# Self attention values with high and low probabilities in one matmul of 512 columns, bank halves added on VectorE, and both queries ahead of the projections

## The reference

```python
q = (x @ wq.T).reshape(b, l, NH, HD)
k = (x @ wk.T).reshape(b, l, NKV, HD)
v = (x @ wv.T).reshape(b, l, NKV, HD)
q = apply_rope(q, freqs_cos, freqs_sin)
k = apply_rope(k, freqs_cos, freqs_sin)
k_full = jnp.concatenate([k_sel, k[0]], axis=0)     # 16 * 32 cached rows and 64 new ones: 576 keys
v_full = jnp.concatenate([v_sel, v[0]], axis=0)
scores = jnp.einsum('bhld,bhtd->bhlt', qh, k_full) / math.sqrt(HD)
attn = jax.nn.softmax(scores, axis=-1)
out = jnp.einsum('bhlt,bhtd->bhld', attn, v_full)
return out.transpose(0, 2, 1, 3).reshape(b, l, NH * HD) @ wo.T
```

## Time and profile before

| | |
|---|---|
| median of 3 runs | 2754.13 us |
| lowest, highest | 2749.89, 2757.01 us |
| the profiled execution | 2757.09 us |
| its span on the core | 2755.3 us |
| mean granted TensorE clock | 0.992 of full speed |
| instructions in the trace | 64145 |
| matmuls, weight loads | 26496, 26496 |
| of them in the self attention's values (L1954) | 13824 each |
| VectorE, ScalarE, GpSimd busy | 1998.2 us (73%), 1538.0 us (56%), 1621.8 us (59%) |

### The profile page before, as it was taken

How to read it: one execution, slowest core, us unless ns; L and a number is a source line. 1 busy time by engine, 2 the same in 40 slices (tenths; PEclk the granted TensorE clock), 3 DMA queues, 4 the chain that set the end, 5 groups by cost and what they waited for, 6 DMA issues and landing times.

```text
span 2755.3 us, 64145 instructions
## 1 busy us (share of the span) xinstructions
PE 2695.3 (98%) x26496; PEld 2374.7 (86%) x26496; DVE 1998.2 (73%) x4005; ACT 1538.0 (56%) x3207; POOL 1621.8 (59%) x1379
## 2 busy tenths in 40 slices
PE   6999999999999999999999999999999999999997
PEld 6888988998888888888888888888888888888876
DVE  5666666666666676666666678887778878777887
ACT  5566666666666566655656655554445455444445
POOL 6887887888777667666667763233334433333235
PEclk8999999999999999999999999999999999999998
DMA  5233233323325312322231331111112111111111
GB/s 172 80 81 106 85 86 100 96 71 104 108 61 166 91 48 80 87 70 77 80 91 44 86 101 43 35 54 35 47 38 64 50 43 39 50 35 43 31 31 62
DMA packets 91484, 197.71 MB, mean 72 GB/s; under 512 B 20664, under 2 KB 21304, under 8 KB 89144
## 3 DMA queue, kind: packets, MB, share of 16 engines
q1 hardware_dynamic: 71480, 154.80, 20.3%
q10 hardware_dynamic: 17664, 34.61, 3.9%
q0 software_dynamic: 2048, 4.20, 0.5%
HBM read 176.78 MB, written 16.78 MB: 70 GB/s over the span
## 4 chain that ended last, share of the span: by engine, by line
PE 89%; DVE 6%; POOL 2%; ACT 2%; issue 1%; DMA 0%; ACTq 0%; DVEq 0%
PE big L1862 30%; PE bank L1862 30%; PE big L1934 14%; PE bank L1954 12%; PE big L1954 3%; DVE nmx L1417 1%; DVE P L1423 1%; PE big L1855 0%; POOL ptl L799 0%; DVE xol L1514 0%; POOL oTl L804 0%; DVE P L1687 0%; DVE rall L1439 0%; DVE qTl L1412 0%; ACT P L972 0%
## 5 line engine op out<-in xcount | busy, mean ns | idle before, releaser
L799 POOL TENSOR_TENSOR ptl<-P,pth 128x576 fp32r<-128x576 f32 x512 | 724.8, 1434 | 240.2 <-ACT pth L981 239.4
L972 ACT ACTIVATE P<-big,nmx 128x576 f32<-128x576 f32 x512 | 378.5, 739 | 406.2 <-DVE nmx L1417 406.0
L1423 DVE STREAM_TRANSPOSE P<-P 128x576 f32<-128x576 f32 x512 | 387.8, 767 | 150.2 <-ACT P L972 148.0
L1954 PE MATMUL bank<-pth,v 32*128 32x256 f32 x4608 | 424.5, 281 | 4.6 <-DVE xacc L1445 1.7
L1954 PE MATMUL big<-pth,v 32*128 32x256 f32 x4608 | 424.6, 281 | 0.0
L1954 PEld LDWEIGHTS bank<-pth,v 32*128 32x128 f32 x4608 | 384.2, 187 | 17.0 <-issue 14.2
L1417 DVE TENSOR_REDUCE nmx<-big 128x1 f32<-128x576 f32 x512 | 373.3, 747 | 6.6 <-PE big L1934 4.8
L981 ACT ACTIVATE pth<-P 128x576 fp32r<-128x576 f32 x512 | 347.7, 682 | 51.0 <-DVE P L1423 50.7
L1954 PEld LDWEIGHTS big<-pth,v 32*128 32x128 f32 x4608 | 363.2, 187 | 0.0
L880 POOL TENSOR_TENSOR P<-P,sm 128x512 f32<-128x512 f32 x64 | 67.3, 1051 | 486.9 <-DVE sm L1716 486.9
L1954 PE MATMUL bank<-ptl,v 32*128 32x256 f32 x2304 | 351.5, 278 | 0.0
(11 more groups left out here) (283 smaller groups left out, 8014.6 us busy)
## 6 DMA issues: line engine op xcount, KB each, us to landing
rall<-kept_r ACTq DMA_DIRECT2D x64, 512.0 KB, 3.7
raw<-in_wo SPq DMA_DIRECT2D x64, 256.0 KB, 3.4
raw<-in_xWq SPq DMA_DIRECT2D x64, 256.0 KB, 2.8
raw<-in_xWo SPq DMA_DIRECT2D x64, 256.0 KB, 2.8
raw<-in_wq SPq DMA_DIRECT2D x62, 256.0 KB, 3.0
v<-kept_v SPq DMA_DIRECT2D x24, 448.0 KB, 7.3
v<-kept_v SPq DMA_DIRECT2D x68, 128.0 KB, 3.4
raw<-in_xWkv SPq DMA_DIRECT2D x32, 256.0 KB, 2.9
```

Of the source, the lines that this page charges most:

```text
L799: pool.tensor_tensor(third_columns(ptl, i), blocks_of(i), f(third_columns(pth, i)), ALU.subtract).then_inc(p_low(i), 1)
L972: act.activation(P[:, i % PSLOTS, :].rearrange("p (k n) -> p k n", k=2), ps_s[i % 2][:, :, 0:HALF], ACT.Exp, bias=nmx[:, i % 8:i % 8 + 1], ...
L1423: dve.transpose(P[:, i % PSLOTS, :], P[:, i % PSLOTS, :]).then_inc(p_turned(i), 1)
L1954: m = pe.matmul(ps_o[a][:, 0:256], v[r, s, l, :], p[r, lo:hi + 1:hi - lo, block_of(b), :, :], start=first, stop=final)
```

## The change

It has four parts.

1. **Probabilities.** `pth` and `ptl` become halves of one tile `pt` [128, 2, 3, KB, 4, 32]. A block now takes two rounds: the high values times high and low probabilities at once, 512 columns, a whole bank; and the low values times the high probabilities, 256 columns, into the bank's first half. 144 matmuls and weight loads a group instead of 216, with the same number of columns.
2. **Adding the halves.** A new step `sum_out(k, a)` on VectorE reduces the two halves of bank a to 256 columns in a new tile `osum` (two slots), and frees the bank (signal `o_sum`). `normalise_out` then reads `osum` and `rall`, both in SBUF.
3. **Room.** `VSLOTS` goes from 22 to 20, so `VEARLY` from 4 to 2: 16 blocks are late instead of 14.
4. **Order.** PE does query 1 and score 7 ahead of projection 0, scores 8' and 9' around projection 1, and the small task between projections 2 and 3. ScalarE does exponential 5 ahead of the high parts of outputs 2 and 3, the query's high parts earlier, exponential 7 after high part 6 and query high 1. VectorE does maxima 4 and 5 between the sums and normalisations, query low 1 before add 0. GpSimd's order and SP's are as they were.

```diff
 GROUPS = 64
-VSLOTS = 22
+VSLOTS = 20
 VEARLY = VSLOTS - KB
...
-            pth, ptl = pair("pt", [128, 3, KB, 4, 32], one)
+            pt = sb("pt", [128, 2, 3, KB, 4, 32], F32R, one)
+            pth, ptl = pt[:, 0], pt[:, 1]
             qTh, qTl = pair("qT", [128, 2, 512], one)
             oh, ol = pair("oT", [128, 2, 512], one)
             rall = sb("rall", [128, 8, 128], F32, one)
+            osum = sb("osum", [128, 2, 2, 4, 32], F32, one)
...
                     out_hi(k, 1)
                 if after:
                     exponent(8 * (k + 1) + 4)
+                if after:
+                    exponent(8 * (k + 1) + 5)
                 if now:
                     out_hi(k, 2)
                     out_hi(k, 3)
+                if later:
+                    query_hi(k + 2, 0)
                 if after:
-                    exponent(8 * (k + 1) + 5)
                     turned_hi(8 * (k + 1) + 4)
                     turned_hi(8 * (k + 1) + 5)
-                if later:
-                    query_hi(k + 2, 0)
                 if 0 <= g < G - 1 and c == 2:
                     values_hi(g + 1)
                 if after:
...
-            def normalise_out(k, a):
+            def sum_out(k, a):
+
                 gate.wait_ge(pv_done, k)
                 gate.wait_ge(in_r, k)
-                dve.tensor_tensor(rall_quarter(a), ps_o[a][:, 0:256].rearrange("p (u t j) -> p u t j", u=2, t=4),
-                                  rall_quarter(a), ALU.mult).then_inc(o_norm((k, a)), 1)
+                both = ps_o[a].rearrange("p (l u t j) -> p u t j l", l=2, u=2, t=4)
+                if k >= 1 or a >= 2:
+                    gate.wait_ge(o_norm, (k, a - 2) if a >= 2 else (k - 1, a + 2))
+                dve.tensor_reduce(osum[:, a % 2], both, AX.X, ALU.add).then_inc(o_sum((k, a)), 1)
+
+            def normalise_out(k, a):
+                gate.wait_ge(o_sum, (k, a))
+                dve.tensor_tensor(rall_quarter(a), osum[:, a % 2], rall_quarter(a), ALU.mult).then_inc(
+                    o_norm((k, a)), 1)
...
-                        normalise_out(k, a)
+                    sum_out(k, 0)
+                    sum_out(k, 1)
+                    normalise_out(k, 0)
+                    normalise_out(k, 1)
+                if after:
+                    maximum(8 * (k + 1) + 4)
+                if now:
+                    sum_out(k, 2)
+                    sum_out(k, 3)
+                if after:
+                    maximum(8 * (k + 1) + 5)
+                if now:
+                    normalise_out(k, 2)
+                    normalise_out(k, 3)
                 if k == GROUPS - 1:
...
 
+            p_rows = pt.rearrange("p h s b t j -> p h s (b t j)")
...
-                    out_place(a, (o_norm, (k, a)))
+                    out_place(a, (o_sum, (k, a)))
                 lo, hi = sorted((slot(k, 0), slot(k, 1)))
                 for b in range(KB):
                     s = (KB * n + b) % VSLOTS
-                    for j, (l, p) in enumerate(((0, pth), (1, pth), (0, ptl))):
+                    o = 128 * block_of(b)
+                    for l in range(2):
                         for a in range(4):
                             r = slice(32 * a, 32 * a + 32)
-                            first, final = b == 0 and j == 0, b == KB - 1 and j == 2
-                            m = pe.matmul(ps_o[a][:, 0:256], v[r, s, l, :], p[r, lo:hi + 1:hi - lo, block_of(b), :, :], start=first,
-                                          stop=final)
+                            first, final = b == 0 and l == 0, b == KB - 1 and l == 1
+                            p = p_rows[r, 0:2 - l, lo:hi + 1:hi - lo, o:o + 128]
+                            m = pe.matmul(ps_o[a][:, 0:512 - 256 * l], v[r, s, l, :], p, start=first, stop=final)
                             if final and a == 3:
                                 m.then_inc(pv_done(k), 1)
...
                     query(k + 2, 0)
                 if after:
                     score(8 * (k + 1) + 6)
+                if later:
+                    query(k + 2, 1)
+                    score(8 * (k + 1) + 7)
                 if now:
                     project(k, 0)
-                if after:
+                if after and not later:
                     score(8 * (k + 1) + 7)
+                if later:
+                    score(8 * (k + 2))
                 if now:
                     project(k, 1)
-                if later:
-                    score(8 * (k + 2))
-                if later:
-                    query(k + 2, 1)
-                for a in task(k):
-                    small_task(*a)
```

52 lines of the change are left out of this document (25 added, 27 removed).

## The result

The changed kernel takes 2781.08 us (median of 4 runs, 2775.78 to 2782.99) against 2754.54 us for the kernel before: a ratio of 1.0099, 95% interval 1.0084 to 1.0113, so 26.5 us slower. The prediction was 2770 us, slower.

A forecast was written before the change was run, and what follows sets the result against it. PE, busy 98% of the span, was taken to bound the kernel. Terms -12.5 + 19.3 + 5.4 + 4.8 + 1.3 - 2.4 = +15.9 us gave 2770 us against the median of 2754.1; range 2746 to 2788.

The forecast's parts named there:

- forecast A: The prediction itself: slower, with GpSimd late in the gathering groups as main loss; 2770 us, own range 2763 to 2778, chance 0.47.
- Rival B: GpSimd is late in the gathering groups, but the shared port is harmless: 2760 us, chance 0.19.
- rival C: In the values, weight loads rather than columns pace PE, and a third are gone: faster, 2739 us, chance 0.16.
- Rival E: In the values, long rounds save only by the gap of 2.5 ns, the rest as forecast A: 2780 us, chance 0.05.
- term 1: Values on PE: merged rounds save 0.24 us a group, in 52 of 64 groups, -12.5 us.
- Term 3: GpSimd's low parts start 1.95 us later behind ScalarE's exponential 5; PE waits in twelve gathering groups, +19.3 us.
- Term 2: VectorE's four new adds take a step of 0.60 us and cost PE nothing, with 0.5 us to spare.
- rival D: VectorE's adds are slow, at a step of 1.13 us, and PE waits: some +90 us, 2840 us, chance 0.13.
- Term 4: VectorE's normalisations of two SBUF tensors wait for GpSimd: +5.4 us in value gatherers, +4.8 in groups 29, 30, 31, 61.
- term 5: Ends: +1.3 us after the last values, -2.4 us in group 1, nothing for the smaller value ring.

The follow-up runs named there:

- Experiment 5: The changed kernel with two of the four gathers moved on GpSimd between output low 1 and output low 2: 2753.88 us, ratio 1.0010.
- Experiment 2: The changed kernel with normalisations 2 and 3 again ahead of maximum 5, and high parts of outputs 2 and 3 ahead of exponential 5: 2786.7 us.
- experiment 3: The changed kernel's new order with the values and normalisation of the kernel before, without adds, ring at 20 slots: 2742.34 us, ratio 0.9964.
- experiment 7: The kernel before with one VectorE edit, the add of projection 3 ahead of transposition 9: 2745.39 us, ratio 0.9983.
- experiment 9: The changed kernel without its four adds, normalisation reading only the first half of each bank from PSUM (output incomplete): 2735.78 us, ratio 0.9948.
- experiment 6: The changed kernel with GpSimd's split of the output weights moved between output low 1 and output low 2: 2779.51 us, ratio 1.0104.
- experiment 1: The changed kernel with the four gathers on GpSimd moved from ahead of low part 6 to behind low part 7: 2778.29 us, ratio 1.0099.
- experiment 11: The changed kernel with all four gathers on GpSimd moved behind low part 9, the last of a group's turn: 2806.33 us, ratio 1.0195.

## Why the prediction was right, and where it was wrong

**The bound and the main term.** The forecast A came true in its places and its sign. That GpSimd would be late by about two microseconds, in these twelve groups and in no plain one, and that PE would wait for it in front of the values, is what the trace shows. By group: 25.62 against 25.7 predicted for group 19, 27.18 within 26.9 to 27.9 for group 17. Experiment 5, which only puts two gathers into GpSimd's idle gap, gives back 1.7 of the 2.2 us in the groups that gather values and all of it in the others. The time of 2781 us lies in the range of 2746 to 2788, but 3 us above A's own 2763 to 2778. Rival B falls with the normalisations of 0.7 to 1.7 us below, rival C with values that take 6.63 us and not under 6.0. Rival E gave 2780, the nearest number, and its mechanism is nearly right (term 1); but its number stands on the rest of A's sum, so that it hits is luck.

**Term 3, its cause.** The step that failed is the sentence that ScalarE's exponential 5 ahead of the high parts of outputs 2 and 3 decides. Experiment 2 took it back and GpSimd's low part 4 stayed where it was. I had laid out the outputs' chain, found it late, and stopped; transposition 4 (1517.40, 11.76 into the group, 9.77 before) and its high part were just as late, for the adds ahead of them and for the query's high part, which the change put ahead of high part 4. That second reason delays low part 4 by 0.83 us even without adds (experiment 3); with them it starts at 13.82, 2.09 later than before. No experiment puts the query's high part back alone. Two chains were late together, and taking one away gains nothing.

**Term 1.** The sum of -0.24 us for a plain group was near the measured -0.36, by two errors. The rounds of 512 columns:

```profile
1506.10 0.40 PE L1977 MATMUL bank<-pt,v 32*128 32x512 f32 x2
...
1506.34 0.28 PE L1977 MATMUL bank<-pt,v 32*128 32x256 f32 x2
...
1506.45 0.40 PE L1977 MATMUL bank<-pt,v 32*128 32x512 f32 x1
```

In the mean of groups 33 to 59 the long round takes 0.236 us, the short one 0.118, together 0.354 against three of 0.120 before. The gain is 6 ns a block and 0.11 us a group, not 0.24. The row of the whole array (0.227) did not carry over to row tiles. The rule of the Trainium skill cited beside this term (TensorE: Matmul & The Clock Gate, Back-to-back issue gap) would have given, as an estimate, 0.045 us a group (18 x 2.5 ns); it and the rows each missed by a factor of more than two, to either side. The rest, 0.25 us, came from the order, to which I had given nothing: experiments 3 and 7.

**Term 2.** The adds cost what was taken:

```profile
1512.33 1.29 DVE L1446 TENSOR_REDUCE osum<-bank 128x256 f32<-128x512 f32 x2 [2.45 <-PE big L1977]
1513.54 0.75 DVE L1450 TENSOR_TENSOR rall<-osum,rall 128x256 f32<-128x256 f32 x2
...
1517.40 1.43 DVE L1426 STREAM_TRANSPOSE P<-P 128x576 f32<-128x576 f32 x2
```

Two sums in 1.29 us, so a step of 0.60, in spite of the stride (rival D falls). Exponential 7 ends at 18.05 (18.2 predicted) and the last projection is added at 23.51 (23.6). In plain groups they cost PE nothing, as said: 24.09 us with them and without (experiment 9).

**Term 4, the port.** The mechanism is right, its size in the value gatherers was not: normalisation 0 takes 0.70 us there instead of 0.42, 0.28 where I took 0.9, since low part 3 ends at 8.3 and not 8.7. So 1.7 us came of the 5.4. Groups 29 to 32 and 61 are 3.8 us longer than before, for 4.8 predicted, but that is near by luck: in experiment 9, without the adds, each takes 24.09 us, so the new order alone would have gained 4.1 there, and the adds with the port cost 7.9. Group 29 (start 800.87), VectorE and then GpSimd:

```profile
808.76 2.01 DVE L1450 TENSOR_TENSOR rall<-osum,rall 128x256 f32<-128x256 f32 x2
```

```profile
807.50 3.00 POOL L802 TENSOR_TENSOR pt<-P,pt 128x576 fp32r<-128x576 f32 x2
810.45 1.61 POOL L807 TENSOR_TENSOR oTl<-rall,oTh 128x256 fp32r<-128x256 f32 x2
```

The pair of normalisations ends at 810.77 where 809.5 was due: the second waits for the end of low part 3, at 810.5. The rule of the Trainium skill on the shared port, cited there, is borne out by experiment 6: where GpSimd's work moves, another normalisation waits (0.71 us instead of 0.42). Before, with one operand in PSUM, none of the 256 normalisations took over 0.43 us.

**What was missed.** First, group 62: it has two more splits on GpSimd, like 61, and I left it out of the list. Both its normalisations take 1.6 us or more, and with no query left to cover it PE waits for exponential 4 (time line of PE):

```profile
1616.38 0.53 PE L1953 MATMUL big<-kTh,qTh 128*128 128x288 f32 x2 [4.26 <-ACT P L975]
```

This wait was 1.26 us before, and the next one, ahead of the first projection, grew from 1.66 to 2.31: +3.7 us. The other 1.8 us of the group's +5.5 are the clock, which these stretches show (the wait, then what follows it; PEclk is 1.00 and 0.50; the header stands in the next fence):

```profile
1612.10:1616.30 4.20, 0.02 (x1) 0.00 (x0) 4.20 (x5) 1.64 (x4) 3.95 (x4) 1.00 0.34 92
1617.00:1623.50 6.50, 4.19 (x13) 3.29 (x12) 3.76 (x7) 4.69 (x10) 4.93 (x5) 0.50 0.00 0
```

Second, the clock elsewhere. In three of the six groups behind value gathers, after a wait of 2.1 us in front of the values, the values run at half speed for some 3 us. Stretches of group 5 and 6, with PE's busy time behind the sum and the granted clock as the column PEclk:

```profile
core 0: us, PE busy (x) PEld busy (x) DVE busy (x) ACT busy (x) POOL busy (x), PEclk, DMA share, GB/s
203.90:205.90 2.00, 0.00 (x0) 0.00 (x1) 2.00 (x4) 0.54 (x1) 2.00 (x3) 1.00 0.94 320
205.90:207.00 1.10, 1.10 (x24) 0.99 (x28) 0.87 (x2) 1.10 (x4) 1.10 (x1) 1.00 0.13 48
207.00:210.00 3.00, 3.00 (x48) 2.65 (x44) 0.78 (x2) 2.27 (x5) 3.00 (x4) 0.53 0.00 0
```

PE stood idle for 2 us and 1.1 us after it went on the clock is at its lower level (0.53 in the mean; 1.2 of 2.4 GHz is 0.50). It costs 1.5 us each time, +4.5 in this trace. The waits of 1.46 us in the key gatherers were followed by it in none of six cases. Over all traces, waits of 1.8 to 2.3 us in front of values were followed by it in 12 of 22 cases, those of 1.4 to 1.5 us in none of 18; what picks the 12 is open. Third, term 5. The wait of 2.6 us in group 1 is gone, but GpSimd's low part now makes PE wait 2.25 us at its end, for group 1 gathers values too; the group is 0.7 us longer where 2.4 less were predicted. After the last values the wait for the output low parts grew by 2.0 us (1.44 to 3.48) and not 1.3, and half clock comes there as well (0.50 from 1640.9 to 1647.5).

**The sum.** Predicted +15.9; in the traces +24.1 from the first values on. The twelve groups that gather: 24.7 predicted (19.3 and 5.4), 20.0 measured. Groups 29 to 32 and 61: 4.8 and 3.8. The end: 1.3 and 2.8. Plain groups, start and the rest: -14.9 (-12.5 and -2.4) and -12.5. The clock (4.5) and group 62 (5.5) had no term. That makes 10.0 us too little; the other lines together are 1.8 too high, so the sum was 8.2 us short. That the total came so near is in part luck, since misses lie on either side. The other 2.4 us by which the medians differ more than the traces no trace shows.

## What to carry to other kernels

When a step gets longer on an engine with idle time, follow everything queued behind it to each engine that waits in order, and price the queue's last item, not the first late one you find: here two chains were late together, and repairing one changed nothing. Look for idle gaps in the order of the late engine before giving up a change: two gathers moved into a gap of 2 us were worth about 25 us. And read the two lines around each handover of the engine that bounds, even where the list of waits is empty: 0.15 us in each of 42 groups, from one add behind one transposition, was more than the 0.11 us that the merged matmuls gained in a plain group. Last, a short wait of the engine that bounds can cost more than itself: look at the granted clock behind it.

## What the runs showed of the hardware that was not expected

- A round of four row-tile matmuls costs 0.118 to 0.120 us at 256 columns and 0.236 at 512, with 8 weight loads less in every 24: merging two rounds saved some 6 ns.
- An idle stretch of PE of 1.8 to 2.3 us in front of the values was followed by half clock in 12 of 22 cases, one of 1.4 to 1.5 us in none of 18.
- A reduction on VectorE that adds the halves of a PSUM bank, 1 KB apart, takes 0.69 us with a step of 0.60, no more than what the prediction took from a contiguous 512-column operation.
- PE stopped inside the values for 13.1 us in 25 places, for nothing that the profile shows, when four gathers started about 2 us ahead of the values, beside the load of the inverse sums (experiment 1). It stopped nowhere in them when the gathers started 4 us behind their start (experiment 11). The cause is open.
- With one split moved on GpSimd, 12 value loads went out 6.6 us later in SP's queue (experiment 6, group 31), though no load had been moved.
